# Sixteen-head attention in a Flamingo block: parts stored as they are made, first operands on two queues, weight-only products beside the first maxima

## The reference

```python
# layer 0: 16 heads
v, k, q = values @ Wv.T, keys @ Wk.T, layernorm(x) @ Wq.T        # as heads of 16 columns
out = softmax(q k^T / sqrt(256)) v;   x = x + tanh(g) * (out @ Wo.T + bo)
# layer 1: the weights of q, k, v are W + B @ A with A of 16 rows
Q = query @ Q_weight.T + (query @ Q_A.T) @ Q_B.T      # K, V alike
```

## Time and profile before

| | us |
|---|---|
| median of 3 runs | 3559.53 (3559.08 to 3561.53) |
| the profiled execution | 3567.27 |
| its span, first to last instruction | 3565.6 |
| projection, to the last store's issue | 0 to 246 |
| first load of the attention | 254.07 |
| first maxima product | 274.41 |
| first score product | 320.43 |
| TensorE busy over the span | 3337.2 (94%) |
| mean granted clock | 0.966 |

### The profile page before, as it was taken

One profiled execution on the slowest core, in us unless ns is written; L12 is line 12 of the kernel. 1 busy time (PEld: TensorE's weight loads), 2 busy tenths in 40 slices (PEclk: granted clock), 3 DMA queues, 4 the chain that ended last, 5 costly groups with the idle time before them and its releaser, 6 DMA issues. The chain is left out here.

```text
span 3565.6 us, 61753 instructions
## 1 busy us (share of the span) xinstructions
PE 3337.2 (94%) x21900; PEld 1995.5 (56%) x21900; DVE 2441.4 (68%) x5488; ACT 1551.6 (44%) x2750; POOL 272.5 (8%) x379
## 2 busy tenths in 40 slices
PE   7978999999999999679959999969999999999999
PEld 4643222222222222568834454438898988898988
DVE  4537989888898985520123444349888888888885
ACT  4533888888888888112211222213222222222221
POOL 0013110101101110110010000000000000000000
PEclk9986999999999999879979999989999999999999
DMA  5678656565565640511121122040000000000000
GB/s 206 258 245 101 85 71 91 72 84 77 79 85 72 88 68 6 186 59 39 36 79 61 61 81 77 31 154 10 12 10 12 10 12 9 13 9 12 10 10 10
DMA packets 144179, 239.89 MB, mean 67 GB/s; under 512 B 22808, under 2 KB 100224, under 8 KB 143488
## 3 DMA queue, kind: packets, MB, share of 16 engines
q1 hardware_dynamic: 134768, 220.67, 29.2%
q0 software_dynamic: 4608, 12.59, 1.1%
q10 hardware_dynamic: 4624, 4.46, 0.4%
HBM read 170.38 MB, written 66.86 MB: 67 GB/s over the span
## 5 line engine op out<-in xcount | busy, mean ns | idle before, releaser
L682 DVE TENSOR_REDUCE at_pmax<-at_psm 128x2 f32<-128x1024 f32 (+1 forms) x832 | 945.3, 1179 | 130.2 <-PE at_psm L513 125.3
L619 ACT ACTIVATE ring<-at_pss 128x512 f32<-128x512 f32 (+1 forms) x1664 | 895.8, 596 | 191.9 <-PE at_pss L537 189.0
L537 PE MATMUL at_pss<-at_qs,at_ks 99*128 99x512 bf16 (+1 forms) x1664 | 511.7, 386 | 12.7 <-ACT ring L619 6.8
L1698 PE MATMUL mt_psd<-mt_xl,mt_key_in 128*128 128x128 f32 x4096 | 491.0, 278 | 2.4 <-DMA mt_key_out<-m_out 2.4
L1698 PEld LDWEIGHTS mt_psd<-mt_xl,mt_key_in 128*128 128x128 f32 x4096 | 469.6, 193 | 3.8 <-DMA mt_key_out<-m_out 2.5
L1724 PE MATMUL mt_psu<-mt_key_out,mt_g 128*128 128x256 f32 x2048 | 447.4, 379 | 1.3 <-DVE mt_g L1934 1.3
L545 PE MATMUL at_pso<-ring,at_vw 128*32 128x512 f32 (+1 forms) x3328 | 443.6, 605 | 0.0
L1724 PEld LDWEIGHTS mt_psu<-mt_key_out,mt_g 128*128 128x128 f32 x2048 | 386.7, 190 | 52.6 <-DVE mt_g L1934 1.4
L537 PEld LDWEIGHTS at_pss<-at_qs,at_ks 99*128 99x128 bf16 (+1 forms) x1664 | 116.4, 98 | 485.5 <-ACT ring L619 425.3
L1786 ACT ACTIVATE mt_g<-mt_psd 128x512 f32<-128x512 f32 x256 | 152.9, 598 | 351.1 <-PE mt_psd L1698 350.7
L511 PE MATMUL at_psm<-at_ks,at_qs 64*128 64x512 bf16 (+1 forms) x1024 | 272.6, 344 | 15.1 <-DVE at_pmax L682 9.9
(11 more groups left out here) (219 smaller groups left out, 3881.4 us busy)
## 6 DMA issues: line engine op xcount, KB each, us to landing
at_ks<-k_dram SPq DMA_DIRECT2D x192, 200.1 KB, 6.8
k_dram<-pj_kp SPq DMA_DIRECT2D x24, 800.5 KB, 5.4
v_dram<-pj_v SPq DMA_DIRECT2D x8, 1664.0 KB, 9.1
at_vd<-v_dram SPq DMA_DIRECT2D x32, 416.0 KB, 10.3
pj_ctx<-ctxT SPq DMA_DIRECT2D x8, 1601.0 KB, 11.7
at_kh<-k_dram SPq DMA_DIRECT2D x128, 100.1 KB, 5.6
aw_ctxT<-ctxT SPq DMA_DIRECT2D x8, 1601.0 KB, 7.2
at_qs<-q_dram SPq DMA_DIRECT2D x192, 64.0 KB, 7.0
```

Of the source, the lines that this page charges most:

```text
L537: nc.tensor.matmul(ps_s[0:r, score_slot(u, n), :], ks[:, g, j, kt * P:kt * P + r], qs[:, g, j, :], start=True, stop=True).then_inc(s_mm, 1)
L619: nc.scalar.activation(pr[0:r, (NST * g + n) % PRING, :], ps_s[0:r, score_slot(u, n), :], ACT.Exp, scale=SCALE).then_inc(expd, 1)
L682: nc.vector.tensor_reduce(heads, found, AX.X, ALU.max).then_inc(m_red, 1)
L1698: ins = nc.tensor.matmul(ps_d[:, j % 2, y * P:y * P + P], key_in[:, k, j * YB + y, :], xl[:, s, k, :], start=k == 0, stop=k == KC - 1)
```

## The change

1. In the projection SP stores a batch's K parts as soon as K is done, then V and the next context load, and Q's parts when they are done.
2. The eight `kh`, `qh` transfers of unit 0 are issued by ScalarE's queue; SP issues the other twelve. The sixteen with parts 0 to 3 count on the semaphore `consts`, and the first maxima product waits for these alone; the first scores wait for the other four.
3. The weight-only products follow the maxima jobs: 34 slots (26 jobs of unit 0, 8 of unit 1), each a job and `beside(slot)`: q, k, v (slots 0 to 2), the two mixes in halves (3 to 6), two key products in each of slots 7 to 11, one in each of 12 to 33. They are written to `ps_o`, one bank for all. The weight is added by TensorE, as a product with the identity, and ScalarE does the copying out. The turn of unit 0's maxima comes behind slot 27; its bank and the score banks move on by one.

```diff
                 def step(i, s, load):
                     b = i * PB + s
-                    sp.wait_ge(third, (b + 1) * NCH)
+                    def parts_out(n):
+                        for part in range(3):
+                            sp.dma_start(t[n + "_dram"][b, part].rearrange("(m p) n -> p m n", p=P),
+                                         parts[n][:, s, part, :, :]).then_inc(stored[s], 16)
+                    sp.wait_ge(third, b * NCH + NKC)
+                    parts_out("k")
                     sp.wait_ge(v_out, (b + 1) * KT + 2)
-                    for part in range(3):
-                        sp.dma_start(t["k_dram"]... ; sp.dma_start(t["q_dram"]...
                     sp.dma_start(t["v_dram"]...
                     if load: ...
+                    sp.wait_ge(third, (b + 1) * NCH)
+                    parts_out("q")
...
+        mix_at = ps_o[:, :].rearrange("p (m d) -> p m d", d=D)
+        def operands_in(g, n, used):
+            return t["consts"] if not used and g == 0 and n < MAX_PARTS else kq_in[g]
+        def low_in(eng, b, g, n, used):    # ks and qs of pair n
+        def high_in(eng, b, g, n, used):   # kh and qh of pair n
+        def operands_there(eng, b, g):
+            if b == g == 0:
+                eng.wait_ge(t["consts"], t["consts_n"] + 16 * 4 * MAX_PARTS)
+            else:
+                eng.wait_ge(kq_in[g], (b + 1) * 16 * NLOAD - (16 * 4 * MAX_PARTS if g == 0 else 0))
...
+                    for n in range(len(Q_PART)):            # SP, load
+                        low_in(sp, b, g, n, used)
+                        if n < MAX_PARTS and (used or g > 0):
+                            high_in(sp, b, g, n, used)
...
                 def low_rank(n, name):
+                    pe.wait_ge(mixed_out, n)
                     left_, right = t["low"][name]
                     for m in range(KC):
-                        ins = nc.tensor.matmul(ps_m[:, n % 2, m, 0:D], right[:, m * P:m * P + P], left_, start=True, stop=True)
+                        nc.tensor.matmul(mix_at[:, m, :], t["ident"][:, :], t["wgt"][name][:, m, :], start=True, stop=False)
+                        ins = nc.tensor.matmul(mix_at[:, m, :], right[:, m * P:m * P + P], left_, start=False, stop=True)
                     ins.then_inc(mixed, 1)
...
-                low_rank(0, "q")
-                low_rank(1, "k")
-                low_rank(2, "v")
-                mix(3, full["q"], full["k"])
-                mix(4, full["v"], t["wgt"]["oT"])
-                pe.wait_ge(mixed_out, 5)
+                PREPARE = len("qkv") + 2 * KC
+                def beside(slot):
+                    if slot < 3:
+                        low_rank(slot, "qkv"[slot])
+                    elif slot < 3 + KC:
+                        mix(3, full["q"], full["k"], slot - 3)
+                    elif slot < PREPARE:
+                        mix(4, full["v"], t["wgt"]["oT"], slot - 3 - KC)
+                    else:
+                        n = slot - PREPARE
+                        for i in range(n + min(n, DOUBLE), n + 1 + min(n + 1, DOUBLE)):
+                            key_product(i)
+                DOUBLE = PREPARE + MH * len(halves) - NJ - EARLY        # 5
...
                 for n in range(NJ):
-                    key_product(n)
                     max_product(0, 0, 0, n)
-                for n in range(NJ, MH * len(halves)):
-                    key_product(n)
+                    beside(n)
                 for n in range(MBANKS):
                     max_product(0, 1, 1, n)
-                pe.wait_ge(k_out, len(halves))
+                    beside(NJ + n)
+                pe.wait_ge(k_out, SBANKS - 1)
                 turn_max(0)
                 for n in range(MBANKS, EARLY):
                     max_product(0, 1, 1, n)
+                    beside(NJ + n)
+                pe.wait_ge(k_out, len(halves))
+                pe.wait_ge(kq_in[0], 16 * (NLOAD - 4 * MAX_PARTS))
                 first_scores(0, 0)
...
             def _(act):
+                for n in range(MAX_PARTS):
+                    high_in(act, 0, 0, n, False)
+                for n, dst in enumerate([full[name] for name in "qkv"] + [t["amat"], t["cmat"]]):
+                    act.wait_ge(mixed, n + 1)
+                    nc.scalar.activation(dst[:, :, :], mix_at, ACT.Copy).then_inc(mixed_out, 1)
                 for n, (m, c) in enumerate(halves):
                     act.wait_ge(k_mm, n + 1)
                     nc.scalar.activation(t["mk"][:, m, c * 512:c * 512 + 512], ps_s[:, n % SBANKS, :], ACT.Copy).then_inc(k_out, 1)
...
             def _(dve):
-                for n, name in enumerate("qkv"): ... tensor_tensor(full[name], ps_m[...], t["wgt"][name], ALU.add)
-                for n, dst in enumerate((t["amat"], t["cmat"])): ... tensor_copy(dst, ps_m[...])
```

More of the change, by code:

```diff
@@ L364, in score_slot @@
     def score_slot(u, n):
-        return (1 + u * (NST + 1) + n + (n > TURN_BEHIND)) % SBANKS
+        return (2 + u * (NST + 1) + n + (n > TURN_BEHIND)) % SBANKS
     def turn_slot(u):
-        return ((u - 1) * (NST + 1) + TURN_BEHIND + 2) % SBANKS if u else 0
+        return ((u - 1) * (NST + 1) + TURN_BEHIND + 3) % SBANKS if u else 1
     with Stage(nc, "at") as st:
@@ L400, in attend_heads @@
             sem(f"at_{n}") for n in ("own", "acc_out", "o_ready", "o_stored", "ones", "inverted"))
+        def operands_in(g, n, used):
+            return t["consts"] if not used and g == 0 and n < MAX_PARTS else kq_in[g]
+        def low_in(eng, b, g, n, used):
+            rows = slice(g * HG * DH, (g + 1) * HG * DH)
+            arrived = operands_in(g, n, used)
+            eng.dma_start(ks[n * DH:(n + 1) * DH, g, :, :],
+                          t["k_dram"][b, K_PART[n], rows].rearrange("(j d) n -> d j n", d=DH)).then_inc(arrived, 16)
+            eng.dma_start(qs[n * DH:(n + 1) * DH, g, :, :],
+                          t["q_dram"][b, Q_PART[n], rows].rearrange("(j d) n -> d j n", d=DH)).then_inc(arrived, 16)
+        def high_in(eng, b, g, n, used):
+            rows = slice(g * HG * DH, (g + 1) * HG * DH)
+            high = slice(MAX_ROWS + n * DH, MAX_ROWS + (n + 1) * DH)
+            arrived = operands_in(g, n, used)
+            eng.dma_start(kh[high, g, :, :], t["k_dram"][b, K_PART[n], rows].rearrange("(p j d) n -> d p j n", j=2, d=DH)
+                          [:, :, 1, :]).then_inc(arrived, 16)
+            eng.dma_start(qh[high, g, :, :], t["q_dram"][b, Q_PART[n], rows].rearrange("(p j d) n -> d p j n", j=2, d=DH)
+                          [:, :, 1, :]).then_inc(arrived, 16)
+        def operands_there(eng, b, g):
[3 more added lines that the diff above has]
+                eng.wait_ge(kq_in[g], (b + 1) * 16 * NLOAD - (16 * 4 * MAX_PARTS if g == 0 else 0))
         with nc.Block() as block:
@@ L409, in load @@
                         sp.wait_ge(pv, (u + 1 - SLOTS) * NST + PRING)
[L410 to L421, removed]
+                    for n in range(len(Q_PART)):
+                        low_in(sp, b, g, n, used)
+                        if n < MAX_PARTS and (used or g > 0):
+                            high_in(sp, b, g, n, used)
                     sp.wait_ge(v_dense_used, u + 1)
@@ L465, in low_rank, with mix @@
                 def low_rank(n, name):
-                    if n == 2:
-                        pe.wait_ge(mixed_out, 1)
+                    pe.wait_ge(mixed_out, n)
                     left_, right = t["low"][name]
                     for m in range(KC):
-                        ins = nc.tensor.matmul(ps_m[:, n % 2, m, 0:D], right[:, m * P:m * P + P], left_, start=True, stop=True)
+                        nc.tensor.matmul(mix_at[:, m, :], t["ident"][:, :], t["wgt"][name][:, m, :], start=True, stop=False)
+                        ins = nc.tensor.matmul(mix_at[:, m, :], right[:, m * P:m * P + P], left_, start=False, stop=True)
                     ins.then_inc(mixed, 1)
-                def mix(n, left_, right):
+                def mix(n, left_, right, m):
                     pe.wait_ge(mixed_out, n)
[L477 to L481, removed]
+                    for k in range(KC):
+                        ins = nc.tensor.matmul(mix_at[:, m, :], left_[:, k, m * P:m * P + P], right[:, k, :],
+                                               start=k == 0, stop=k == KC - 1)
+                    if m == KC - 1:
+                        ins.then_inc(mixed, 1)
                 def key_product(i):
@@ L647, in _ @@
                 dve.sem_inc(m_red, MBANKS)
[L648 to L652, removed]
-                    nc.vector.tensor_copy(dst[:, :, :], ps_m[:, (n + 3) % 2, :, 0:D]).then_inc(mixed_out, 1)
                 def invert(u, me, piece):
```

6 lines of the change are left out of this document (1 added, 5 removed).

## The result

| | before | after |
|---|---|---|
| median of 22 runs each, us | 3561.43 | 3566.69 |
| ratio, 95% interval | | 1.0013 (1.0007 to 1.0018) |
| the profiled execution, us | 3567.27 | 3564.26 |
| last Q part done to first load | 14.9 | 4.3 |
| first load to first maxima product | 20.3 | 13.8 |

The forecast was 3549.6 us with a range of 3543 to 3557, counted from a median of 3559.53; with more runs the kernel before stands at 3561.43. The whole change is 5.3 us slower in the medians: within 0.2%, outside the range, and on the other side. (The last Q part is done at 236.00 here and at 239.18 before. Over the seventeen traces of this document it is done between 235.9 and 239.9, with either order of the stores, hence the distances.)

What follows compares the result with a forecast made beforehand. The first score product was taken to wait for the later of the maxima chain (310.5) and the load backlog (309.8). 310.5 against 320.4 is 9.9 us less, giving 3549.6 us from the median 3559.5; range 3543 to 3557.

Steps and rivals of the forecast that it cites:

- Stores: End of projection: only Q's 768 KB wait, so loads begin 4.3 us after 239.2, 10.6 us earlier.
- First operands: First load to first maxima product: 1585 KB at one rate, 15.8 us; 11.2 if side by side.
- side-by-side one: Unit 0's operand loads: two queues double the rate of their common part; 3545.0 us, chance 0.30.
- Weight-only products: Slots from first maxima to last key product: 45.0 us with full clock from 5 us on, 57.0 at half clock.
- the late clock: Rival: TensorE's clock rises only with slot 6, 5 us more, 3554.6 us; chance 0.14.
- a clock that never rises: Rival: TensorE stays at half clock, slots take 57.0 us, 3561.6 us, slower; chance 0.09.
- ScalarE's hold: ScalarE copies the turned maxima only after the fourth key half; chain A ends 6.2 us behind the last key product.
- The chain's sum: Chain A to the first score: 243.5 + 15.8 + 45.0 + 6.2 = 310.5, against 320.4 before.
- The point it was counted from: First score at 320.4 us in the profiled execution before; its gain of 9.9 was taken off the median 3559.5.
- the backlog: Chain B, SP's queued loads ahead of unit 0's rows: 66.3 us from first load, first score 309.8 after the change.
- chain A: Operands, maxima, turn, split, rows ahead of the first score; alone it would allow 312.9 before, 310.5 after.

Runs made afterwards that it cites:

- The clock given: Whole change plus thirty identity products, results unused, run in the operand wait; ratio to the kernel before 0.9998, medians -2.2 us.
- products moved: Kernel before with only the weight-only products moved beside the maxima jobs, stores and loads as before; ratio 1.0049, medians +17.1 us.
- rows on ScalarE's queue: Kernel before with unit 0's three row transfers issued by ScalarE instead of SP; ratio 1.0021, medians +7.5 us.
- parts 1 and 2 with load 2 late: Kernel before with early stores, first operands on two queues, and unit 2's loads issued behind unit 0's rows; ratio 0.9953, medians -17.8 us.
- part 1 alone: Kernel before with only the projection's stores reordered as in the change; ratio 0.9966, medians -10.5 us.
- part 2 alone: Kernel before with only unit 0's operands on two queues and the first maxima waiting for parts 0 to 3; ratio 0.9998, medians -0.7 us.
- load 2 late: Kernel before with SP issuing unit 2's loads behind unit 0's row transfers; ratio 1.0000, medians +0.6 us.

## Why the prediction was wrong

**Stores: right.** 4.3 us against 14.9, and 10.5 us in the medians when it is alone.

**First operands: right within its bounds.** 13.4 to 14.2 us where nothing else holds the first maxima, between 15.8 and 11.2. The rate while both queues run is 138 to 167 GB/s; it was 123. The Trainium skill ("SBUF — State Buffer", "Can I just issue two DMAs to hit both halves?") gives 6% more for two transfers at once, at partitions 0 and 64; here it is 12 to 36%, so the measurement decides, on a value between its rule and the side-by-side one. Whether the second queue or the other half of the partitions gives it, no run here separates.

**Weight-only products: the step that failed.** It said "I take full clock from 5 us on" and so 45.0 us; it was 55.8, and all of the difference lies in slots 0 to 6 (26.0 for 15). The failed argument is that a stretch without a gap "is nearer to the rows that rose". TensorE's shown busy time did not tell when the clock would rise: at 2.85 to 3.00 of 3 us it stayed at 0.50 for 25 us, through maxima, identity, low-rank and mix products, and over the products of the operand wait it rose in five traces and not in four. By the prediction's own prices slots 0 to 6 are 23.0 at half clock in place of 15: 8 us are the clock. The other 3 are a second wrong term, the price of a product: 0.86 holds between products of one kind. Where an identity product and a 16-row product alternate it is 1.15, and in the mixes two products between maxima jobs take 2.0. Both are 0.86 each with some 0.3 more for every run of one kind, of which slots 0 to 2 have four each and slots 3 to 6 one; the waits for ScalarE's copies, 0.2 where 0.51 was counted, gave 1 us back. Slots 0 to 2 took 15.9 us where 3 x (0.54 + 3.43 + 0.51) = 13.4 would be at half clock by the terms of the sum. The rival with the right mechanism was the late clock ("with slot 6"), but its price, 5 us, was too low: those same 8 and 3 are 11. So even with the rise the slots came near the 57.0 of a clock that never rises. The clock given (48.2) and the identity products taken out (46.0) recover 6 to 8 and 8 to 10 us; both causes are shown, and they overlap, so they do not add.

**ScalarE's hold: right.** 6.6 us behind the last key product (6.2 counted); without it, 6 to 7 us less.

**The chain's sum.** Q's end plus 4.3 + 15.8 + 45.0 + 6.2 = 71.3 was forecast and 4.3 + 13.8 + 55.8 + 6.6 = 80.5 measured: 9.2 late, against 81.2 before. By the traces alone the whole change should gain 0.7 us.

**The point it was counted from: probably wrong too.** The sum took the 320.4 of one profiled execution, held there by the backlog, as the time of every execution. That what moves the first score moves the attention's end is borne out: from the first score to the attention's last product all seventeen traces take 1112.5 to 1114.3 us. But the stages behind it, the same instructions in all kernels, take 2132 to 2144 us, so the time of a single execution says little about this stretch, and the traces are better set against medians. In all fifteen pairs of a changed kernel with before (fourteen in the table, and the first), the difference of medians is the trace's score less 76.8, within 3.6 us, thirteen of them within 1.9: products moved +17.9 and +17.1, whole change +3.7 and +5.3, then +2.4 and +2.4, rows on ScalarE's queue +7.1 and +7.5, parts 1 and 2 with load 2 late -16.9 and -17.8. The 76.8 is fitted, as the mean of score less difference over the fifteen, and each difference has an interval of 2 to 5 us either way. It should be the score of before in a median execution, but its two traces stand at 80.4 and 81.2.

The simple reading is that in most executions of before the wait for the backlog is some 4 us shorter than in its two traces; chain A alone would allow 7.5 less. For it: part 1 alone, behind the same backlog, gained 3.6 us more in the medians than by its trace. Against it: part 2 alone, with such a backlog too, gained only 0.8 more, and "load 2 late", which has no backlog to wait for, should gain 2.9 and shows +0.6. So the 4 us are inferred from pairs of trace and median, no trace shows them, and their reason stays open.

So: -9.9 as forecast, + 9.2 for the chain (+ 10.8 for slots, - 2.0 for operands, + 0.4 for the hold), + 4.4 for the reference, gives +3.7, where +5.3 and +2.4 were measured. By the traces of before alone, without the last term, the change should have gained 0.7 us: the 9.2 are enough to undo the forecast, whatever the reference is.

## What to carry to other kernels

Work that fills a wait costs nothing there; before it is spread over a later, bound stretch, price it at the slow clock and at the price of alternating kinds of product, for the clock may not rise when TensorE looks busy. When a chain is shortened, look for what arrives just behind it: here a queue's backlog took 1 to 3 of the 5 to 7 us by which the second queue brought the rows forward, and 5 to 6 more came free once loads that nobody yet needed were issued behind the small transfer on the path. And before a gain is counted from the end of a wait in one profiled execution, hold it against several traces and medians: the wait may be shorter in the others.

## What the runs showed of the hardware

- **The clock.** Thirty products with one 128-row weight tile back to back: 1.00 from 246 on, about 5 us behind the first. Maxima pairs (64 rows) with identity, 16-row and mix products, gaps of 0.15 us at most: 0.50 for 25 us, then 1.00 at 280 to 286, and 0.50 again from 289, though TensorE was shown busy for 3.00 of 3 at 295 (before at 275 to 302 too). And one series of products with gaps of 0.74 to 0.79 was granted 1.00 towards its end in five traces and stayed at 0.50 in four. The Trainium skill ("TensorE: Matmul & The Clock Gate", Part 1) ties the clock to how busy the array has been; the first case agrees, and in the second the profile's busy time was no measure of it.
- **fp32 products.** With 256 columns at half clock, 0.86 us each, and some 0.3 more for every run of one kind: two between maxima jobs 2.0, four that alternate (128 rows, 16 rows) 4.6. Products over 16 rows in different partitions (q from 0, k from 32) and different banks ran side by side: four in 2.08 us, as long as two.
- **A small transfer behind a backlog.** 4 KB land in 1.7 us with the DMA engines free, and the slowest of three in 8.5 to 12.1 us with loads of later units pending, from the same queue or another. The Trainium skill ("DMA: Bandwidth & Descriptors", Queues, rings and completion order) lets each DMA engine take turns between queues packet by packet, and lets a completion wait for earlier writes of that engine across queues. By the first alone I would have expected ScalarE's rows early, and they were not; whether the second accounts for the 11 to 12 us, no run here isolates.
